# Direct rows written with d outermost, folded twice by GpSimd, and the remaining quarter summed by VectorE

## What is computed

```python
e = stack([tbl_f[ids[:, f]] for f in 32 fields], axis=1)      # B=1024, F=32, D=32
h = x = e
for W, b in ((W0, b0), (W1, b1), (W2, b2)):                   # 128, 128 and 1 outputs
    z = relu(einsum('bhd,bmd,ohm->bod', h, x, W) + b)
    # layers 0 and 1: the first 64 outputs go on as h, the last 64 are "direct"
    # layer 2: its one output is direct
z = sum(concatenate(directs), over d)                          # B x 129
h = concatenate([z, dense_ctx])                                # B x 145
h = relu(h @ W_top1 + b_top1); h = relu(h @ W_top2 + b_top2)
y = h @ W_top3
```

## Time and profile before

| | |
|---|---|
| median of 3 runs | 1181.52 us (1180.07 to 1185.25) |
| time of the profiled execution | 1183.08 us |
| its span, first to last instruction | 1181.2 us |
| TensorE busy | 1126.7 us, 95% |
| VectorE busy | 1082.9 us, 92% |
| ScalarE busy | 460.0 us, 39% |
| GpSimd busy | 514.5 us, 44% |

### The profile page before, as it was taken

The page is one execution under the profiler, slowest core; times in us unless marked ns, Lnnn a source line. Parts: engine busy times, 40 slices in busy tenths (PEclk is TensorE's granted clock), DMA queues, the critical chain, the costliest instruction groups (busy, mean ns, idle before and its releaser), DMA issues.

```text
span 1181.2 us, 10957 instructions
## 1 busy us (share of the span) xinstructions
PE 1126.7 (95%) x3608; PEld 652.1 (55%) x3608; DVE 1082.9 (92%) x604; ACT 460.0 (39%) x383; POOL 514.5 (44%) x270
## 2 busy tenths in 40 slices
PE   0789999999999999999999999999999999999998
PEld 0345555555555555556555555555556555555554
DVE  1599999999999999999999999999999999999973
ACT  0234444433444433344443334444333444443424
POOL 6604444555444455544445554444555444450000
PEclk9999999999999999999999999999999999999999
DMA  7744443454545344454434455443445544333100
GB/s 222 222 138 133 137 152 121 118 139 137 159 137 142 121 126 136 140 157 138 140 118 130 127 148 148 147 138 120 132 127 148 154 141 142 128 120 112 54 0 1
DMA packets 63413, 154.94 MB, mean 131 GB/s; under 512 B 12753, under 2 KB 29394, under 8 KB 63394
## 3 DMA queue, kind: packets, MB, share of 16 engines
q1 hardware_dynamic: 37202, 96.64, 23.2%
q10 hardware_dynamic: 18000, 53.85, 17.3%
q0 software_dynamic: 8192, 4.21, 3.6%
HBM read 95.79 MB, written 8.39 MB: 88 GB/s over the span
## 4 chain that ended last, share of the span: by engine, by line
DVE 36%; issue 23%; ACT 11%; ACTq 11%; PE 9%; DMA 9%; DVEq 1%; SPq 1%
DVE prod L398 13%; DVE prod_lo L444 12%; DVE raw L437 9%; PE z_ps L530 8%; ACTq L726 5%; ACT prod_hi L753 5%; ACTq L727 5%; DMA x_roll<-x_dram 4%; ACT h_roll L716 4%; DMA x_part<-x_dram 4%; ACT direct L720 1%; DVE raw L420 1%; DVE lo L427 1%; PE mlp_ps L530 1%; SPq L349 1%
## 5 line engine op out<-in xcount | busy, mean ns | idle before, releaser
L530 PE MATMUL z_ps<-prod,w_sb 128*128 128x512 f32 x1536 | 696.5, 600 | 48.1 <-issue 28.4
L303 POOL DMA_INDIRECT gathered<-in_table,rows_sb x256 | 509.9, 1992 | 522.1 <-DVE h2x L451 451.5
L530 PEld LDWEIGHTS z_ps<-prod,w_sb 128*128 128x128 f32 x1536 | 288.5, 191 | 367.2 <-issue 335.0
L753 ACT CAST prod_hi<-raw 128x2048 fp32r<-128x2048 f32 x128 | 244.1, 1907 | 424.4 <-DVE raw L437 365.8
L444 DVE TENSOR_TENSOR prod_lo<-raw,prod_hi 128x2048 fp32r<-128x2048 f32 x128 | 292.3, 2284 | 26.5 <-ACT prod_hi L753 26.5
L437 DVE TENSOR_TENSOR raw<-h_roll,x_roll 128x2048 f32<-128x2048 f32 x128 | 292.7, 2287 | 3.3 <-DMA h_roll<-h_roll 0.9
L398 DVE TENSOR_TENSOR prod<-h_roll,x_roll 128x2048 f32<-128x2048 f32 x128 | 292.5, 2285 | 0.0
L530 PE MATMUL z_ps<-prod_hi,w_hi 128*128 128x512 f32 x520 | 214.9, 493 | 3.0 <-DVE prod_lo L444 3.0
L530 PE MATMUL z_ps<-prod_hi,w_lo 128*128 128x512 f32 x520 | 164.2, 395 | 0.0
L530 PE MATMUL z_ps<-prod_lo,w_hi 128*128 128x512 f32 x520 | 164.1, 395 | 0.0
L398 DVE TENSOR_TENSOR prod<-x_base,x_roll 128x2048 f32<-128x2048 f32 x63 | 143.4, 2287 | 15.1 <-DMA x_roll<-x_dram 8.4
(11 more groups left out here) (56 smaller groups left out, 231.9 us busy)
## 6 DMA issues: line engine op xcount, KB each, us to landing
x_roll<-x_dram SPq DMA_DIRECT2D x128, 512.0 KB
x_base<-x_dram SPq DMA_DIRECT2D x32, 512.0 KB
h_roll<-h_roll ACTq DMA_DIRECT2D x32, 448.0 KB, 3.4
h_roll<-h_roll ACTq DMA_DIRECT2D x32, 384.0 KB
h_roll<-h_roll ACTq DMA_DIRECT2D x32, 320.0 KB
x_dram<-gathered SPq DMA_DIRECT2D x64, 128.0 KB
h_roll<-h_roll ACTq DMA_DIRECT2D x32, 192.0 KB
h_roll<-h_roll ACTq DMA_DIRECT2D x33, 128.0 KB
```

The lines of the kernel that those rows point to most:

```text
L303: nc.gpsimd.indirect_dma_start(gathered[:, u, g * DIM:(g + 1) * DIM], None, table, bass.IndirectOffsetOnAxis(ap=rows_sb[:, col:col + 1], a ...
L530: return nc.tensor.matmul(*args, **kw)
L753: nc.scalar.copy(prod_hi[:, b % SPLIT_RING, :, :], raw[:, :, :]).then_inc(hi_ready, 1)
```

## The change

ScalarE writes each direct row with d outermost: the instructions of lines 720 and 740 read PSUM in its order and write column (r, d) to column (d, r), so that neighbouring writes lie 32 floats (128 bytes) apart. `direct` has four slots instead of two, and `relu0` waits for the sum of chunk c-4. GpSimd folds a chunk's slot in place: it adds columns 512 to 1023 to columns 0 to 511 (`fold_direct`), then columns 256 to 511 to columns 0 to 255 (`fold_again`), which halves the number of d values twice. In GpSimd's program the two folds of a chunk stand just ahead of the eight gathers that use the same place u of the next group. VectorE then sums 8 values of d for each row instead of 32, from 256 columns whose d values lie 32 floats apart, and does so at b = 3 of the step instead of b = 1. The last chunk isn't folded: VectorE sums all its 32 values, 32 floats apart.

```diff
-        direct = sb("direct", [P, 2, CHUNK])
+        direct = sb("direct", [P, UNROLL, CHUNK])
...
+            def fold_direct(u, done):
+                d = direct[:, u, :]
+                pool.wait_ge(ids_loaded, 32)
+                pool.wait_ge(direct0_ready, done)
+                pool.wait_ge(direct1_ready, done)
+                nc.gpsimd.tensor_tensor(d[:, 0:CHUNK // 2], d[:, 0:CHUNK // 2], d[:, CHUNK // 2:CHUNK], ALU.add
+                                        ).then_inc(direct_halved, 1)
+
+            def fold_again(u, halved):
+                d = direct[:, u, :]
+                pool.wait_ge(ids_loaded, 32)
+                pool.wait_ge(direct_halved, halved)
+                nc.gpsimd.tensor_tensor(d[:, 0:CHUNK // 4], d[:, 0:CHUNK // 4], d[:, CHUNK // 4:CHUNK // 2], ALU.add
+                                        ).then_inc(direct_quartered, 1)
+
+            make_rows(0)
+            for u in range(UNROLL):
+                gather(u, 1, 0)
+            with pool.Fori(0, CHUNKS // UNROLL - 1) as group:
+                done = [settled(pool, group * UNROLL + u + 1) for u in range(UNROLL)]
+                made = settled(pool, group + 2)
+                make_rows(group + 1)
                 for u in range(UNROLL):
+                    fold_direct(u, done[u])
+                    fold_again(u, done[u])
+                    gather(u, made, done[u])
+            for u in range(UNROLL - 1):
+                fold_direct(u, CHUNKS - UNROLL + u + 1)
+                fold_again(u, CHUNKS - UNROLL + u + 1)
...
             def sum_direct(c, u, group):
-                dve.wait_ge(direct0_ready, c + 1)
-                dve.wait_ge(direct1_ready, c + 1)
+                if is_last(c):
+                    dve.wait_ge(direct0_ready, c + 1)
+                    dve.wait_ge(direct1_ready, c + 1)
+                else:
+                    dve.wait_ge(direct_quartered, c + 1)
+                parts = DIM if is_last(c) else DIM // 4
...
-                                        direct[:, u % 2, :].rearrange("p (q r d) -> p q r d", q=QUADS, d=DIM),
+                                        direct[:, u, 0:parts * ROWS].rearrange("p (d q r) -> p q r d", d=parts, q=QUADS),
                                         AX_X, ALU.add).then_inc(direct_summed, 1)
...
-                    if b == 1 and not_first(c):
+                    if b == 3 and not_first(c):
                         sum_direct(c - 1, (u - 1) % UNROLL, group if u else group - 1)
...
-                wait(act, direct_summed, c - 1)
-                nc.scalar.activation(direct[0:HID, s, :], z0_ps[HID:P, :], ACT.Relu,
+                wait(act, direct_summed, c - UNROLL + 1 if not_first(c, UNROLL) else 0)
+                nc.scalar.activation(by_dim(direct[0:HID, u, :]), by_row(z0_ps[HID:P, :]), ACT.Relu,
...
-                nc.scalar.activation(direct[HID:P, s, :], z1_ps[HID:P, :], ACT.Relu,
+                nc.scalar.activation(by_dim(direct[HID:P, u, :]), by_row(z1_ps[HID:P, :]), ACT.Relu,
```

More of the change, by code:

```diff
@@ L227, in build_tower @@
         h2x_ready = sem("h2x_ready")
+        direct_halved = sem("direct_halved")
+        direct_quartered = sem("direct_quartered")
         direct_summed = sem("direct_summed")
@@ L282, in _, with make_rows @@
             pool.wait_ge(ids_loaded, 32)
-            def gather_group(group):
+            def make_rows(group):
                 cols = UNROLL * GATHERS
-                made = settled(pool, group + 1)
-                freed = [0 if isinstance(group, int) else settled(pool, (group - 1) * UNROLL + u + 1)
-                         for u in range(UNROLL)]
                 for u in range(UNROLL):
@@ L293, in gather_group, with gather @@
                                         ALU.add).then_inc(rows_made, 1)
+            def gather(u, made, freed):
                 pool.wait_ge(ids_loaded, 32)
                 pool.wait_ge(rows_made, made)
-                for u in range(UNROLL):
[L299 to L306, removed]
@@ L308, in _ @@
-            gather_group(0)
-            with pool.Fori(1, CHUNKS // UNROLL) as group:
-                gather_group(group)
+                wait(pool, h2x_ready, freed)
+                for g in range(GATHERS):
+                    col = u * GATHERS + g
+                    nc.gpsimd.indirect_dma_start(
+                        gathered[:, u, g * DIM:(g + 1) * DIM], None, table,
+                        bass.IndirectOffsetOnAxis(ap=rows_sb[:, col:col + 1], axis=0),
+                    ).then_inc(gather_done[u], 16)
@@ L706, in _, with by_row, by_dim @@
             act.dma_start(top_b[1:1 + DENSE, :], dense_t).then_inc(mlp_loaded, 16)
+            def by_row(tile):
+                return tile.rearrange("p (r d) -> p r d", d=DIM)
+            def by_dim(tile):
+                return tile.rearrange("p (d r) -> p r d", d=DIM)
             def relu0(c, u):
```

## The result

| | before | after |
|---|---|---|
| median | 1182.08 us (1180.07 to 1185.25, 4 runs) | 1213.16 us (1212.61 to 1215.14, 4 runs) |
| ratio, 95% interval | | 1.0263 (1.0237 to 1.029) |
| span of the profiled execution | 1181.2 us | 1211.0 us |

The kernel became 31 us slower (25 us in a later series of runs, reported with the last experiment). I had forecast 1189 us within 1183 to 1212: the sign was right, the size was a quarter of the measured one, and the time lies just outside the range.

The account below looks back on a forecast made before the run. The prediction took ScalarE to bound the leg and VectorE the rest of each step, TensorE close behind. New sum +4.5 and row-number steps +3.4 gave +7.9 us: 1191.0 on the profiled 1183.1, 1189 on the median; range 1183 to 1212.

Parts of the forecast that it names:

- the leg: From `raw` b=1's end to `prod_lo` b=2's start: 11.18 us of ScalarE's work; removing VectorE's old sum there gains nothing.
- The longer ring: Four slots of `direct`: removes nothing, since `relu0`'s write did not wait for the sum before.
- cost on the path: nothing, with 0.44 us to spare: Folds between `raw` b=1 and `prod_lo` b=2: 1.44 us more, 1.13 less, +0.31 us against a mean wait of 0.75.
- the term of +4.5 us: New sum at b=3: 31 sums at 0.33 us, 10.2 us, less 5.7 us taken back by `x_roll` waits.
- The +3.4 us for steps with row numbers: First fold might hit `raw` b=1 in seven steps where GpSimd makes row numbers: 6.7 us, half counted.
- Rival (a): Strided accesses cost about double, new sum about 0.60 us: +12 us, 1194; at the bound +28, 1210. Chance 25%.
- rival (b): The first fold hits `raw` b=1 in every step: +29 us, with the new sum +33, 1215. Chance 8%.
- (c): Folds hold VectorE beyond its slack before `prod_lo` b=2, deciding from 1.88 us per step: +28 us, 1210. Chance 7%.
- (d): The wait at `prod_lo` b=2 is really VectorE's: 0.80 us less per step, up to TensorE's limit, 1170. Chance 10%.
- What would break the argument: A new wait no row shows, above all TensorE waiting for slower direct rows and delaying VectorE through `u_ps`; no size given.

Follow-up runs that it names:

- the last experiment: Unedited changed and before kernels run again; in five further runs the changed kernel took 1212.47 us beside 1187.69 us, ratio 1.0206.
- before, reload held: Kernel before, with SyncE's reload of `x_roll` b=1 waiting for `whole` b=2 instead of `whole` b=1: 1173.66 us, ratio 0.9892.
- change, reload held: Changed kernel, with SyncE's reload of `x_roll` b=1 waiting for `whole` b=2 instead of `whole` b=1: 1188.88 us, ratio 1.0041.
- before, second profile: Kernel before, unedited, profiled once more for its head: 1186.69 us in one run.
- sum moved: Kernel before, with four slots and the full contiguous sum moved from b=1 to b=3, no folds or strides: 1209.11 us, ratio 1.0221.
- short folds: Changed kernel, with each GpSimd fold cut to 32 columns and strided writes kept: 1199.88 us, ratio 1.0114.
- folds added: Kernel before, with GpSimd also folding a scratch tile of zeros at the changed kernel's places: 1220.9 us, ratio 1.0285.
- no strides: Changed kernel, with ScalarE's direct-row writes and the new sum's reads made contiguous, folds kept: 1226.29 us, ratio 1.0361.
- change, second profile: Changed kernel, unedited, profiled once more for its head: 1203.98 us in one run.
- with the issues moved: Changed kernel, with `relu0`'s six transfers issued after `prod_hi` b=2: 1188.81 us, ratio 1.0017.

## Why the prediction was off, point by point

**Right.** The mechanism of the folds: GpSimd waits for VectorE's running instruction and then stretches the next. I had 0.96 and 0.48 us for the two, measured were 1.08 and 0.54. The estimate by the Trainium skill's page "GPSIMD Engine Reference", section 3.1, 1.69 us for both, is closer to the measured 1.62 than my 1.44. The first fold lands on `whole` b=1 in 27 of 30 steps of the first profile and in all 30 of the second. Taking the old sum out of the leg gained nothing (shown by moving it alone), and the wait for `x_roll` swallowed part of the new one. The longer ring gained nothing that shows.

**The step that failed** is "cost on the path: nothing, with 0.44 us to spare", the folds in the leg. I had called the leg "ScalarE's own work and issue" and held its length fixed, and looked only at VectorE's slack in it. But `whole` b=1, which the fold stretches, is also what SyncE waits for to reload `x_roll` b=1, and I hadn't asked what its later end would move. The issues became 0.56 us longer per step, the leg 0.58, where my sum had nothing. The runs put numbers on it:

| kernel | how much later `whole` b=1 lets the reload go | issues | stretch of `raw` b=1 | leg |
|---|---|---|---|---|
| before, reload held | past the issues | 4.28 | 0 | 12.92 |
| change, reload held | past the issues | 4.34 | 0 | 13.18 |
| before | 0 | 4.68 | 0 | 13.30 |
| before, second profile | 0 | 4.79 | 0 | 13.44 |
| sum moved | 0 | 4.73 | 0 | 13.36 |
| short folds | 0.06 | 4.80 | 0 | 13.43 |
| folds added | 0.54 | 5.03 | 1.04 | 14.71 |
| no strides | 0.55 | 5.02 | 1.01 | 14.65 |
| change | about 1.0 | 5.24 | 0 | 13.88 |
| change, second profile | 1.09 | 5.22 | 0 | 13.86 |

All numbers are us; the second column is how much longer `whole` b=1 lasts than 2.28 us. The leg is 8.64 us, ScalarE's own fixed part, plus the issues plus the stretch of `raw` b=1, within 0.05 us in every row but the second, where VectorE's 13.2 us take over. The issues grow with the delay of the reload; the four rows from 4.68 to 4.80 us can't be told apart, since two profiles of the same kernel differ by nearly as much.

The changed kernel's first trace holds the same test by chance. In three of its 30 steps a gather of 11.70 us held GpSimd up until `whole` b=1 had begun, and SyncE's stores and loads came later as well. One of them:

```profile
685.87 11.70 POOL L300 DMA_INDIRECT gathered<-in_table,rows_sb  x1 [0.30 <-issue]
```

```profile
698.99 2.29 DVE L421 TENSOR_TENSOR prod<-h_roll,x_roll 128x2048 f32<-128x2048 f32 x1
701.19 3.38 DVE L467 TENSOR_TENSOR prod_lo<-raw,prod_hi 128x2048 fp32r<-128x2048 f32 x1
```

```profile
704.38 1.73 SPq L372 DMA_DIRECT2D x_roll<-x_dram  x2
```

```profile
703.31 0.52 ACTq L759 DMA_DIRECT2D h_roll<-h_roll  x1
...
704.51 0.89 ACTq L759 DMA_DIRECT2D h_roll<-h_roll  x1
...
707.05 0.63 ACTq L760 DMA_DIRECT2D h_roll<-h_roll  x1
```

The first fold came too late for `whole` b=1 and stretched `prod_lo` b=1 instead, and the reload went out 1.07 us behind the first issue and not 0.79 ahead. Strides and folds are all there, and yet the six issues last 4.37 us. In the other two such steps they last 4.38 and 4.71 us, against a mean of 5.34 in the rest of the 25.

That the reload's timing is the cause is shown, since moving this one wait alone shortens the issues in both kernels; what inside the transfers' path makes an issue last longer is not. Of the 25.9 us by which the steps grew, the legs are 17.8, and nearly all of that is this (against the second profile of the kernel before, whose legs sum to 402.1, it is 14.9).

**Mis-sized**: the new sum, 0.33 taken and 0.51 measured, and what the wait for `x_roll` gives back. I had 5.7 us in 31 steps, 0.18 per step, from the waits as listed; from start to start `products0`'s first instruction takes 2.54 us before and 2.20 after, so it gave back 0.34. The two errors nearly cancel in a mean rest, 0.51 - 0.34 = +0.17 us, and the term of +4.5 us came out at +6.2 in the rests: nearly right by luck. The +3.4 us for steps with row numbers, in which the fold was to hit `raw` b=1, came out at nothing: `raw` b=1 takes 2.29 us in all 30 steps. Rival (a) was right that strides cost, though less than its 0.60 us for the sum: a read of 256 columns 0.51 instead of 0.33 us, and ScalarE's write of 1024 columns 2.12 instead of 1.11. The Trainium skill's page "Advanced Engine Details and Errata", section "SBUF Cachelines", had said so and the trace agrees. I gave it 25% because no row of before had a stride.

**Right for a wrong reason**: that the first fold misses `raw` b=1. I took 0.48 us for GpSimd's response, from a gather; the folds start 0.17 us after the direct rows. With the old write of 1.11 us the fold hits, as the run without strides shows: `raw` b=1 takes 1.01 us more and the leg is 14.65 us instead of 13.88. What saved it is the slower write, which the prediction names only as a remark against rival (b).

**The other rivals**: (c) did not occur, since the folds' 1.62 us stayed below the 1.88 from which it decides; of the kernels with folds only those with the reload held and with the issues moved show a leg that VectorE sets. (d) fell with the sum moved alone.

**What would break the argument** was to be TensorE waiting for slower direct rows and handing that on through `u_ps`. TensorE's wait came, 22.3 us in 24 waits, but `h2x` waited only 3.0 us for `u_ps`, inside the leg, where VectorE had 18.8 us to spare. The slow write isn't needed for it either: with the sum moved alone, and contiguous writes, TensorE waits 17.1 us in 24 waits for the direct rows.

**Not counted on**: the head, +3.8 us in the first profile, -2.4 in the second. In the profile with an early head the changed kernel took 1204 us; in the two in which the first `relu0` begins only at 45 to 47 us, after a wait that the profile can't name, it took 1213. Such a start at 45 us or later occurred in 4 of the 14 profiled executions, once in a kernel that is the one before with ScalarE's issues moved, so it doesn't need the folds (the kernel before with the reload held had such a wait too, a shorter one, and began at 40.17). But the changed kernel had it in two of its three profiles and the unchanged one in neither of its two, so whether the change makes it more frequent stays open.

**Why the idea itself doesn't pay here.** It gives VectorE back 1.13 us and takes 1.62 in stretched instructions and 0.51 in the remaining sum: +1.0 us per step. The pair of kernels with the issues out of the way comes close to it, +1.08. Folds placed where VectorE stands idle weren't tried.

**A version that beats both** is the kernel before with ScalarE's six transfers issued behind `prod_hi` b=2: 1166.47 us, 1.7% faster (0.9826, 0.9796 to 0.9857), with no gap left on TensorE from 500 to 700 us.

## What to carry to other kernels

An addition on GpSimd beside a VectorE that streams two SBUF inputs wasn't free help here: it cost VectorE 2.1 ns per column of the addition, so compare what is saved with what is stretched before anything else. When an instruction gets longer, list everything that its semaphore releases, the transfers of other queues too, and ask what they will run into; slack on its own engine isn't the whole answer. And time spent on issuing transfers is work on a path like any other: put it behind the instruction that someone waits for, and then look at what the transfers now meet, since two such moves that each gain can lose together.

## What the runs showed of the hardware that was not expected

- The time that ScalarE's queue needs to issue the same six transfers ranged from 4.28 to 5.24 us on average, with what else was being transferred. Single issues took from 0.52 to 1.96 us in the changed kernel.
- A stride of 128 bytes made ScalarE's write of 1024 columns 1.9 times as long (2.12 against 1.11 us), and VectorE's sum of 1024 columns 1.6 times (1.92 against 1.21 us, in the last chunk).
- The recorded duration of a GpSimd addition says little: the folds of 512 and 256 columns show 2.5 and 2.6 us and stretched VectorE by 1.08 and 0.54. Much of that is probably waiting: without strides the first fold asked 0.2 us before it could get in and shows 1.32.
- In the changed kernel's first profile four gathers have a recorded duration of 11.70 us each, against about 2 us for the others; none in the two profiles of the kernel before is over 3.1 us. They didn't lengthen their steps: in three of the four the leg was shorter, 13.13 to 13.34 us, as told above.
